# A two-layer graph transformer on one core: layer two's neighbour sums as three bf16 parts, and zero rows, residual rows, expert weights and dense rows moved to other times and queues

## What is computed

```python
# layer one
xn = layernorm(x)
x  = x + gnn0(xn) + mixer0(xn)             # gnn0: sum over edges of (xn @ W_neighbor)[src] * weight
x  = x + top1_of_8_experts(layernorm(x))
# layer two
xn = layernorm(x)
h_src = xn * rsqrt(clip(out_deg, 1))[:, None]
agg   = segment_sum(h_src[src], dst) * rsqrt(clip(in_deg, 1))[:, None]
gnn1  = elu(agg @ weight + bias)
mix1  = linear_attention_block(xn)         # q, k, v; phi; Wo; norm; hidden layer of 1024; norm
x  = x + gnn1 + mix1
x  = x + sum_of_top2_of_8_experts(x)
```

## Time and profile before

| | us |
|---|---|
| median of 3 runs | 3095.96 (3094.58 to 3096.40) |
| the profiled execution | 3084.4 |
| its span | 3082.8 |
| TensorE busy | 2428.9 (79%) |
| VectorE, ScalarE, GpSimd busy | 1182.7, 1085.2, 597.3 |
| granted TensorE clock, mean | 0.879 |

### The profile page before, as it was taken

One profiled execution on the slowest core, in us unless ns is written; L12 is line 12 of the kernel. 1 busy time (PEld: TensorE's weight loads), 2 busy tenths in 40 slices (PEclk: granted clock), 3 DMA queues, 4 the chain that ended last, 5 costly groups with the idle time before them and its releaser, 6 DMA issues.

```text
span 3082.8 us, 39405 instructions
## 1 busy us (share of the span) xinstructions
PE 2428.9 (79%) x11905; PEld 1938.2 (63%) x11906; DVE 1182.7 (38%) x2571; ACT 1085.2 (35%) x2028; POOL 597.3 (19%) x482
## 2 busy tenths in 40 slices
PE   0776799989889798876699557968888897925887
PEld 0444688877768677664588435646666666614776
DVE  4444677754635446332001242323342524230111
ACT  3222577755646556532232221121212111112222
POOL 1610011100100101012122111111313223023554
PEclk9887799999898898977799778978989897957999
DMA  3321011110100201024222233212122212053443
GB/s 121 92 79 55 24 45 43 33 63 31 58 31 18 71 30 60 28 80 111 81 75 65 81 129 106 72 47 70 45 70 58 74 46 78 7 142 67 84 86 63
DMA packets 162717, 202.09 MB, mean 66 GB/s; under 512 B 59801, under 2 KB 131120, under 8 KB 162581
## 3 DMA queue, kind: packets, MB, share of 16 engines
q0 software_dynamic: 75168, 89.11, 12.5%
q1 hardware_dynamic: 75834, 100.45, 9.8%
q10 hardware_dynamic: 11578, 10.82, 1.1%
HBM read 108.51 MB, written 93.74 MB: 66 GB/s over the span
## 4 chain that ended last, share of the span: by engine, by line
PE 42%; DMA 38%; another core or an unknown queue 7%; DVE 4%; ACT 3%; issue 2%; SPq 1%; POOL 1%; ACTq 0%; DVEq 0%; POOLq 0%
PE bank L713 39%; DMA agg_rows<-agg_t 34%; PE bank L719 3%; DMA arena<-agg_rows 1%; POOL w_adj L565 1%; SPq L403 1%; DMA xg<-expert_rows 1%; DMA arena<-in_x 1%; DMA feat<-xg 1%; ACT count_a L1167 0%; ACT w_qc L1167 0%; ACT agg_t L1184 0%; DVE arena L1879 0%; ACT w_adj L1166 0%
## 5 line engine op out<-in xcount | busy, mean ns | idle before, releaser
L713 PE MATMUL bank<-xg,w_adj 125*125 125x256 f32 (+1 forms) x2500 | 656.9, 401 | 0.0
L713 PEld LDWEIGHTS bank<-xg,w_adj 125*125 125x125 f32 x2500 | 458.3, 196 | 64.7 <-issue 1.2
L713 PEld LDWEIGHTS bank<-arena,row_hot 128*125 128x125 f32 x3200 | 423.2, 198 | 88.2 <-issue 68.0
L713 PE MATMUL bank<-arena,row_hot 128*125 128x100 f32 x3200 | 431.0, 281 | 47.1 <-remote 19.6
L719 PE MATMUL bank<-ident,arena 125*128 125x125 f32 (+1 forms) x650 | 139.1, 337 | 338.0 <-remote 178.6
L713 PE MATMUL bank<-t,w_h 128*128 128x250 f32 (+1 forms) x1184 | 325.8, 428 | 17.6 <-remote 11.4
L719 PEld LDWEIGHTS bank<-ident,arena 125*128 125x128 f32 (+1 forms) x650 | 85.1, 167 | 389.3 <-issue 383.2
L1560 DVE TENSOR_TENSOR row_hot<-iota_all,arena 128x2000 f32<-128x2000 f32 x100 | 223.7, 2237 | 224.7 <-PE bank L713 221.8
L1166 ACT ACTIVATE w_adj<-bank 125x200 f32<-125x200 f32 x400 | 217.5, 544 | 259.3 <-PE bank L713 254.0
L713 PEld LDWEIGHTS bank<-t,w_h 128*128 128x128 f32 x1184 | 229.6, 199 | 109.9 <-issue 57.9
L713 PE MATMUL bank<-w_adj,arena 128*125 128x256 f32 x1024 | 241.5, 394 | 0.0
(11 more groups left out here) (322 smaller groups left out, 2939.1 us busy)
## 6 DMA issues: line engine op xcount, KB each, us to landing
count_a<-counts POOLq DMA_DIRECT2D x25, 781.2 KB, 6.3
sorted_in<-pad_rows POOLq DMA_DIRECT2D x16, 878.4 KB, 16.9
arena<-sorted_in SPq DMA_DIRECT2D x49, 251.0 KB
counts<-count_a SPq DMA_DIRECT2D x13, 781.2 KB
counts<-w_qc SPq DMA_DIRECT2D x12, 781.2 KB
arena<-rows_b SPq DMA_DIRECT2D x5, 1875.0 KB
w_adj<-in_L_ffn_Wd POOLq DMA_DIRECT2D x8, 1024.0 KB, 6.2
w_adj<-in_L_ffn_W POOLq DMA_DIRECT2D x16, 512.0 KB, 5.8
```

Source lines behind the costliest of these rows:

```text
L713: return pe.matmul(o, w, r, start=first, stop=last, skip_group_check=not check)
```

## The change

**Sums.** The messages are split into three bf16 parts (their sum is the float value up to rounding): two lie in `xg`, the third in the upper half of `w_adj`. The count blocks are loaded as bf16 straight to where TensorE reads them, without the cast, two ahead. An aggregate is 75 bf16 matmuls of 257, 256 and 256 columns. ScalarE makes the first part, after it has normalised the rows (VectorE did that before) and written the float messages into two staging buffers from which SP stores them; GpSimd makes parts two and three (`message_parts`).

**Layer one's last step.** GpSimd's order was expert weights, scatter, zero rows with a wait for them, scatter, residual load. It is now scatter, zero rows, expert weights, the wait, scatter; the residual load comes after expert 0's results. VectorE does its routing before the out-degrees.

**Layer two's zero rows** are stored by SP ahead of its last aggregate load, their places given at the start of the last mixer step; GpSimd loads the expert weights only after VectorE has received the last aggregate rows.

**First dense rows.** SP loads them ahead of the last query store, inside the projections; `q1` gets a place of its own. In `project1` VectorE's `tails` comes ahead of the wait for the query buffer.

The diff, cut to its core, eight columns of indent taken off:

```diff
+adj1 = [w_adj[0:B, NB * 64 * i:NB * 64 * (i + 1)].bitcast(BF16).rearrange("p (c d) -> p c d", c=NB) for i in range(2)]
+part2 = w_adj[0:B, NB * 128:NB * 256].bitcast(BF16).rearrange("p (c d) -> p c d", c=NB)
+parts = xg[:, 0:NB, :].bitcast(BF16)
+part0, part1 = parts[:, :, 0:D + 1], parts[:, :, D + 2:2 * D + 2]
+stage_all = row_hot[0:B, :, :, :].rearrange("p k j n -> p (k j n)")
+stage = [stage_all[:, G * D * k:G * D * k + G * D].rearrange("p (i d) -> p i d", i=G) for k in range(2)]
+rest = stage_all[:, 2 * G * D:3 * G * D].rearrange("p (i d) -> p i d", i=G)
...
-q1 = cut(2560, 1280).rearrange("p (i n) -> p i n", i=G)
+q1 = count_a[0:B, 0:G * D].rearrange("p (i n) -> p i n", i=G)
...
-        sp.dma_start(rows(feat1, s), xg[:, G * s:G * s + G, 0:D]).then_inc(msg_stored, 16)
+        sp.dma_start(rows(feat1, s), stage[s % 2]).then_inc(msg_stored[s % 2], 16)
...
-    with sp.Fori(0, NS) as s:
+    def queries_out(s):
         take(sp, q_full)
         sp.dma_start(rows(rows_b[:, 2 * D:3 * D], s), q1).then_inc(q_free, 16)
+    def nodes_in(s):
+        take(sp, rowb_used)
+        sp.dma_start(row_b, rows(rows_b, s)).then_inc(rowb_in, 16)
+    with sp.Fori(0, NS - 1) as s:
+        queries_out(s)
+    nodes_in(0)
+    queries_out(NS - 1)
...
-    nodes_in(0)
     with sp.Fori(0, NS - 1) as p:
         aggregates_in(p)
         nodes_in(p + 1)
         result_out(p)
+    take(sp, tails_known)
+    for e in range(E0):
+        tail = sp.value_load(tail_tab[0:1, e:e + 1], min_val=CAP * e, max_val=CAP * e + N - G * B)
+        sp.dma_start(sorted_in[ds(tail, TAIL), :].rearrange("(i p) d -> p i d", p=B),
+                     pad_rows[:, :].unsqueeze(1).to_broadcast([B, TAIL // B, D + 1])).then_inc(pads_stored, 16)
...
-    def counts_in(b):
-        pool.dma_start(flat(count_cur[0]), counts[b * B:b * B + B, :]).then_inc(count_in, 16)
     def adjacency_in(b):
-        pool.wait_ge(count_in, 16 * (b + 1))
         if b >= 2:
             take(pool, adj_used[b % 2])
-        pool.tensor_copy(adj[b % 2], count_cur[0]).then_inc(counts_copied, 1)
-        take(pool, counts_copied)
-        pool.sem_inc(adj_in[b % 2], 1)
-        if b + 1 < NB:
-            counts_in(b + 1)
+        pool.dma_start(flat(adj1[b % 2]), counts[b * B:b * B + B, :]).then_inc(adj_in[b % 2], 16)
+    def message_parts(s):
+        at = slice(G * s, G * s + G)
+        pool.wait_ge(msg_full, s + 1)
+        pool.memset(part0[:, at, D:D + 1], 1.0)
+        chain(pool.tensor_tensor(rest, stage[s % 2], part0[:, at, 0:D], ALU.subtract))
+        chain(pool.tensor_copy(part1[:, at, :], rest))
+        chain(pool.tensor_tensor(part2[:, at, :], rest, part1[:, at, :], ALU.subtract))
+        pool.sem_inc(parts_made, 1)
+        chain.restart()
...
+            if layer == 0 and e == 0:
+                pool.wait_ge(rowx_free, 16)
+                pool.dma_start(h_big, by_part(rows_x)).then_inc(rowx_in, 16)
...
     pool.wait_ge(graph_done, 1)
+    scatter(1, y_ids)
+    zero_tails()
     for e in range(2):
         expert_w(0, e)
+    pool.wait_ge(tails_stored, 16 * E0)
     scatter(1, y_ids)
-    zero_tails(0)
-    scatter(1, y_ids)
-    pool.wait_ge(rowx_free, 16)
-    pool.dma_start(h_big, by_part(rows_x)).then_inc(rowx_in, 16)
     expert_results(0)
     pool.wait_ge(counts_kept, 1)
-    counts_in(0)
-    adjacency_in(0)
-    pool.wait_ge(msg_stored, 16 * NS)
+    for b in range(2):
+        adjacency_in(b)
+    for s in range(NS):
+        message_parts(s)
+    for k in range(2):
+        pool.wait_ge(msg_stored[k], 16 * ((NS + 1 - k) // 2))
...
+    take(pool, last_begun)
     for e in range(2):
         expert_w(1, e)
-    zero_tails(1)
+    pool.wait_ge(pads_stored, 16 * E0)
...
-                take(pe, adj_in[par])
+                landed = nth * 16 + 16
+                pe.wait_ge(adj_in[par], landed if isinstance(landed, int) else pe.snap(landed))
...
-                    mm(ps_agg[0:B, 0:cols], adj[par][:, c, 0:B], xg[:, c, 0:cols], False, False, False)
+                    if layer == 0:
+                        mm(ps_agg[0:B, 0:D], adj[par][:, c, 0:B], xg[:, c, 0:D], False, False, False)
+                    else:
+                        mm(ps_agg[0:B, 0:D + 1], adj1[par][:, c, 0:B], part0[:, c, :], False, False, False)
+                        mm(ps_agg[0:B, 0:D], adj1[par][:, c, 0:B], part1[:, c, :], False, False, False)
+                        mm(ps_agg[0:B, 0:D], adj1[par][:, c, 0:B], part2[:, c, :], False, False, False)
...
-        pe.wait_ge(nodes_full, s + 1)
+        pe.wait_ge(msg_full, s + 1)
...
-            pe.wait_ge(msg_full, NS)
-        aggregate(s, s % 2, 1, total)
+            pe.wait_ge(parts_made, NS)
+        aggregate(s, s % 2, 1, total, nth=s // 2)
...
+        take(act, act_in)
+        act.activation(sd[:, :], mv[:, :, 1], ACT.Sqrt, bias=eps[:, :]).then_inc(act_out, 1)
         act.wait_ge(nodes_full, s + 1)
         for i in range(G):
             b = G * s + i
-            last = act.activation(xg[:, b, 0:D], n_big[:, b, :], ACT.Copy, scale=inv_out[:, b:b + 1])
+            last = act.activation(n_big[:, b, :], h_big[:, b, :], ACT.Identity, bias=shift[:, i:i + 1],
+                                  scale=rs[:, i:i + 1])
         chain(last)
+        if s >= 2:
+            act.wait_ge(msg_stored[s % 2], 16 * (s // 2))
+            act.wait_ge(parts_made, s - 1)
+        for i in range(G):
+            b = G * s + i
+            last = act.activation(stage[s % 2][:, i, :], n_big[:, b, :], ACT.Copy, scale=inv_out[:, b:b + 1])
+        chain(last)
+        chain(act.activation(part0[:, G * s:G * s + G, 0:D], stage[s % 2], ACT.Copy))
         act.sem_inc(msg_full, 1)
...
-        norm(n, h)
+        norm_sums(h)
+        dve.sem_inc(act_in, 1)
+        take(dve, act_out)
+        chain(dve.reciprocal(rs[:, :], sd[:, :]))
+        chain(stt(out=shift[:, :], in0=mv[:, :, 0], scalar=-1.0, in1=rs[:, :], op0=ALU.mult, op1=ALU.mult))
...
+        tails(s, 1)
         take(dve, q_free, 16)
...
+    routes()
     chain(dve.tensor_reduce(inv_out[:, :], deg_all.rearrange("p b (h c) -> p c (b h)", h=2), AX.X, ALU.add))
     chain(ts(inv_out[:, :], inv_out[:, :], 1.0, None, ALU.max))
     root()
     chain(dve.reciprocal(inv_out[:, :], inv_out[:, :]))
-    routes()
...
-    with dve.Fori(0, NS) as s:
+    with dve.Fori(0, NS - 1) as s:
         project1(s)
-        tails(s, 1)
     dve.wait_ge(nodes_stored, 32)
+    dve.sem_inc(rowb_used, 1)
+    project1(NS - 1)
     take(dve, k4_used)
     take(dve, q_free, 16)
     take(dve, sums_full)
     dve.sem_inc(loop_done, 1)
-    dve.sem_inc(rowb_used, 1)
...
         dve.sem_inc(v_full, 1)
+        if plan is LAST:
+            ends()
...
         take(dve, aggs_in, 16)
         if plan is LAST:
-            ends()
+            dve.sem_inc(last_begun, 1)
```

More of the change, by code:

```diff
@@ L258, in program @@
         st2 = sb("st2", [128, 2])
+        eps, shift = sb("eps", [B, 1]), sb("shift", [B, G])
         table_of = sb("table_of", [1, 1])
@@ L293, in program @@
         count_made = pair("counts_made")
-        counts_copied = sem("counts_copied")
-        counts_kept, count_in = sem("all_counts_stored"), sem("counts_loaded")
+        counts_kept = sem("all_counts_stored")
         adj_in, adj_used = pair("adjacency_in"), pair("adjacency_used")
@@ L334, in program @@
         nodes_full, nodes_stored, head_stored = sem("nodes1_full"), sem("nodes1_stored"), sem("nodes1_head_stored")
-        msg_full, msg_stored = sem("messages1_full"), sem("messages1_stored")
+        msg_full, msg_stored, parts_made = sem("messages1_full"), pair("messages1_stored"), sem("message_parts_made")
         step_got = [sem(f"step_rows_loaded{s}") for s in range(NS)]
         aggs_used = sem("step_aggs_used")
+        last_begun, pads_stored = sem("last_step_begun"), sem("pad_rows1_stored")
         tile_ready = sem("normalised_tiles")
@@ L502, in _ @@
                 sp.dma_start(bc[:, i, :], row(a[n])).then_inc(l_bc, 16)
-            def nodes_in(s):
-                take(sp, rowb_used)
-                sp.dma_start(row_b, rows(rows_b, s)).then_inc(rowb_in, 16)
             def aggregates_in(s):
@@ L549, in _ @@
             chain(pool.tensor_copy(ident_b[:, :], ident[:, :]))
+            chain(pool.memset(eps[:, :], LN_EPS))
             chain(pool.memset(xg[:, :, D:D + 1], 1.0))
@@ L615, in gather @@
                         bass.IndirectOffsetOnAxis(ap=idx_tail[:, 0:1], axis=0)).then_inc(tail_full, 16)
-                if layer == 1 and b + 1 < NB:
+                if layer == 1 and 2 <= b + 1 < NB:
                     adjacency_in(b + 1)
@@ L664, in scatter, with zero_tails @@
                             src[:, i, :], None).then_inc(scattered, 16)
-            def zero_tails(layer):
+            def zero_tails():
                 take(pool, tails_known)
@@ L672, in zero_tails @@
                                    pad_rows[:, :].unsqueeze(1).to_broadcast([B, TAIL // B, D + 1])).then_inc(tails_stored, 16)
```

(20 more changed lines are left out.)

## The result

| | before | changed |
|---|---|---|
| median (4 runs each) | 3096.18 us | 2984.6 us (2977.5 to 2994.02) |
| ratio, 95% interval | | 0.9649 (0.9618 to 0.9680) |
| profiled execution, its span | 3084.4, 3082.8 | 2994.02, 2992.4 |

The change saves 111.6 us at the median, and 90.4 us between the two profiled executions. Most of the difference between these two numbers lies ahead of the change: up to the end of layer one's last aggregate the code is the same but for one constant, and the counting matmul right behind it starts at 1362.42 us before and at 1378.63 after. In all traces of this study it starts between 1362.4 and 1379.7. So I compare lengths of stages, not times from the start.

The account below looks back on a forecast made before the run. TensorE's own work was taken to bound the dense stretches, late transfers the still ones. Terms summed to -127.2 on the profiled 3084.4 us, giving 2957.2; the median's 11.6 offset made it 2969, range 2935 to 3025.

Parts of the forecast that it names:

- T1: Into layer two, up to its first aggregate: extra ScalarE steps +4.3 against -2.8 for the aggregate, +1.5 us (-2 to +8).
- T2: First mixer step: earlier dense rows -19.3, shorter sums 2.75 + 1.35 saved, together -23.4 us (-15 to -24).
- Part 1: Price of a layer-two aggregate: 75 bf16 matmuls take 8.4 us instead of 11.13, weight loads hidden.
- rival (a): Weight loads don't hide: an aggregate stays at 11.1 us, its savings of 45 us go, time 3014; chance 10%.
- T0: Layer one's end and its experts: earlier transfers -26.3, residual load delaying expert 2's weights +14; -12 us (-26 to -3).
- near 12: Sign: TensorE's idle ahead of layer one's experts would be near 12 us instead of 32.
- Projections: Layer two's projections: tail ahead of the query-buffer wait -15, three shorter aggregates -7.9, together -22.9 us.
- Middle steps: Four middle steps: shorter sums 6.4 and no cast stall 3.1 us a step, +4 back; -34 us (-22 to -44).
- Last step: Last mixer step: three aggregates -4.4, SP's zero-row issues and VectorE's earlier hand-over +2; -2.4 us (-6 to +5).
- T3: End of layer two: zero rows -20.5, later weights -9, VectorE's slow instructions -5; -34 us (-22 to -36).
- (b): Moved transfers end a wait that something else ends soon after; half of 74 us stays, 3006 to 3035; chance 16%.
- (c): Layer two's granted clock falls from 0.89 to 0.70: +174 us, kernel slower at 3143; chance 2%.

Follow-up runs that it names:

- e7: Changed kernel with message parts two and three summed in their first 64 columns only, 125 weight columns kept: 2996.29 us in one execution.
- e8: Changed kernel with message parts two and three summed in their first 64 columns only, but 128 weight columns: 2987.80 us in one execution.
- f1: Kernel before, with all moved transfers and orders of the change, but float sums, count cast and VectorE's normalisation kept: 3017.51 us, ratio 0.9746.
- e9: Changed kernel with zeros written for message parts two and three instead of subtracting and casting: 2972.43 us in one execution.
- g1: e10 with the first three residual-row stores at layer two's start issued by GpSimd: median 2978.15 us over six runs, ratio 0.9628.
- e4: Changed kernel with VectorE's tail back behind the wait for the query buffer in the projections: median 2997.35 us, ratio 0.9682.
- e5: Changed kernel with the first dense rows loaded after the projections again, behind the bias rows: median 3009.05 us, ratio 0.9735.
- e10: Changed kernel with the residual load behind expert 5's results and layer two's seven bias rows in own memory, loaded before query stores: 2987.16 us, one execution.
- e6: Changed kernel with an unneeded GpSimd cast of 3200 columns after each gather of layer two: 3006.56 us in one execution.
- e3: Changed kernel with layer two's zero rows on GpSimd's queue again, behind the expert weights: median 3019.56 us, ratio 0.9759.

## Why the prediction was right, and where it was off

It gave 2969 for 2984.6, in a range of 2935 to 3025; by the medians 16 us of 127 did not come, by the stages 21. The mechanisms were in the main the forecast ones, save in T1 and T2; most terms were somewhat too large, and some errors cancelled. Its good and bad ends add up to 2935 and 3031 by its own terms, where it has 2933 and 3033. Step by step:

- **Part 1.** 8.4 us forecast, 8.4 measured, and rival (a) fell. One premise did not hold: a load of 125 bf16 columns lasts 138 ns in the trace, longer than the 0.11 us from one matmul to the next. The estimate of 104 ns from the Trainium skill, "TensorE: Matmul & The Clock Gate", section "LDWEIGHTS (loading the stationary operand)", was too low; the measurement decides. The load hides all the same, so the records of neighbouring loads overlap; e7 and e8 put what its 125 columns add to a short matmul at some 15 ns.
- **T0.** The first pair came 13.8 + 7 us earlier by the forecast, 18.8 by the trace; the aggregate rows gave 5.1 instead of 7. TensorE's idle ahead of the experts is 18.40 us, as 32.43 - 13.8 gives; the "near 12" among the signs took the 7 us off this wait too, though they belong to another. The term mis-sized was what comes back: +14 less 5.5 was forecast, 13.1 measured. The weights of expert 2 were late, as forecast: they landed 40 us after their issue, and TensorE's last 9.85 us of waiting are for them. Not in the working were the input rows on SP's own queue, which the load slowed from 4 to 19 us, 7.14 us of waiting one pair earlier. That wait only took its part of the longer one: without it TensorE would have been done with the pair before at 1543.0 by an estimate (1528.39 + 6.91 + 0.59 + 7.07) and have waited some 18 us for weights that landed at 1561.29. Of the two waits, 17.0 us, 5.5 are repaid; the other 1.6 us of the 13.1 fit the matmuls right behind the waits, 8.34 and 9.38 us where 7.07 and 6.91 are usual.
- **T1.** +1.5 against +0.3, by a wrong way. The working took ScalarE's extra steps as the price and let VectorE gain 1.7 us a step; VectorE lost 3 us in three of five steps beside GpSimd instead. It cost nothing, since the stores take as long: f1, without the extra steps of ScalarE and GpSimd, has 97.81, e9 97.98, g1 99.37. The 2.8 us of the first aggregate went into the projections of that step, which now all run behind the gate.
- **Projections.** -24.1 against -22.9, closer than its parts: e4 gives the wait alone as 13.9 where 15 stood, f1 the sums as 10.3 where 7.9 stood. The two errors cancel in part, which is luck.
- **T2.** -19.4 against -23.4. The dense rows gave what was forecast (e5: 19.7 for 19.3). The step that failed is the rest: that no wait would be left ("none at the first mixer step"), so that 2.75 + 1.35 us of sums would show as well. VectorE still waited 11.77 us and TensorE 3.05, for bias rows that stood last in SP's queue (e10: 5.0 us). f1 has T2 2.8 us shorter with float sums: there TensorE waits under 1 us at that turn, since the longer sums cover the wait.
- **Middle steps.** -28.5 against -34. The stall of 3.1 us was right (e6: 3.6 a step). The arithmetic was mis-sized: 6.4 us a step forecast, (31.6 - 4 x 3.1)/4 = 4.8 by f1, and 4.0 by the traces of before and after. One place is known: the part of an aggregate in "ranks" starts behind an idle stretch at a granted clock of 0.50, 0.64 us a chunk for the first eight chunks. It took 7.5, 7.6, 7.2 and 7.1 us in the four steps where 8.6, 9.0, 8.6 and 9.1 stood, 1.5 saved a step and not 2.0. Where the rest went stays open; the granted clock over the four steps was 0.88 before and in f1 and 0.85 now.
- **Last step.** -0.3 against -2.4. The sums are shorter there as well, but VectorE's one-hot tiles for the tails are now last (3.25 and 1.32 us of waiting).
- **T3.** -31.3 against -34, e3 gives 25.7 for the zero rows, where the forecast had 20.5 and 5 for VectorE's slow instructions beside them. The aggregate rows gave 6 of the forecast 9: 7.9 us from issue to VectorE, for 14.1 before.
- **Rivals.** (b) was true in the small: something late next took back 4 us in T2 and 4.6 more in the experts. (c) did not come at its size: the clock was 0.872 over the run for 0.879. Its direction was right, though: with the same moves and float sums (f1) the four executions were granted 0.886 to 0.890, with the bf16 parts 0.871 to 0.878. Why was not tested.

## What to carry to other kernels

A large load on a queue makes everything issued behind it on that queue as late as itself; place it where little stands behind it, and list what that is, scatters too, not only the transfer that one has in mind. Then ask what moves at that time on other queues: here the input rows on SP's took 19 us instead of 4. When a wait is taken away, read which other wait ends at the same instruction, and in which order the waits stand: here bias rows hid behind dense rows, and two limits of nearly equal length made the start of layer two immune to the removal of either. Saved TensorE columns are worth their share only in stretches where TensorE is neither waiting nor coming back from a wait.

## What the hardware showed that was not expected

- A GpSimd operation of 1280 columns with two inputs slows a VectorE add of two SBUF operands from 2.07 to 5.1 us for five, in the same step, and a cast of 3200 columns holds a VectorE instruction of 0.29 us for 3.4. The Trainium skill, "SBUF — State Buffer", section "Who interferes with whom", tells of one port pair that the two engines share and that one of them can hold for a whole instruction. VectorE's instruction beside the cast ends 0.16 us behind it (2097.20 and 2097.04), which agrees.
- GpSimd's queue completed a small scatter 31 us after its issue, with the 3.2 MB load before it, though the DMA engines were busy for a share of only 0.32 (1540 to 1560). The trace explains both. Of the load's 16 completions eleven came at 1530.4 to 1532.1 and five at 1557.2 to 1557.6; the scatter behind it completed in eleven parts by 1538.1 and in five at 1561.0 to 1561.5, and the weights likewise. A share of 0.32 of 16 engines is five. So five engines seem to have carried this load over 125 partitions at 120 GB/s, and what stands behind it is late by those five. Whether another layout of the load would use more of them was not run.
- Making the sums shorter still (e7) did not make the middle steps shorter. The granted clock over them was lower with it, 0.75 for 0.85, and 0.854 for 0.872 over the run. Why was not tested.
